# Delta rule and cross-attention: the gate's projection and Tanh moved among the level products, the state chain's last steps moved ahead of keys and taps, and stacks written whole to DRAM

## The reference

```python
def step(S, inp):
    qt, kt, vt, gt, bt = inp
    S = S * jnp.exp(gt)[..., None]
    vd = (vt - jnp.einsum('bhkv,bhk->bhv', S, kt)) * bt[..., None]
    S = S + kt[..., None] * vd[:, :, None, :]
    return (S, jnp.einsum('bhkv,bhk->bhv', S, qt))
...
q, k, v = (causal_conv_silu(x @ W, conv_w, conv_b) for each of q, k, v)   # 4 taps
g = -exp(A_log) * softplus(x @ Wfa @ Wfb + dt_bias)
q = l2norm(q) * SCALE; k = l2norm(k)
o = kda_scan(q, k, v, g, sigmoid(x @ Wb))
gate = (x @ Wga @ Wgb)
o = o * rsqrt(mean(o * o) + EPS) * o_norm_w * sigmoid(gate)
out = o @ Wo
```

## Time and profile before

| | |
|---|---|
| median of 3 runs | 6407.26 us (6398.27 to 6415.52) |
| the profiled execution | 6422.86 us |
| its span | 6421.3 us |
| PE / DVE / ACT / POOL busy | 78% / 61% / 43% / 32% of the span |
| granted clock of TensorE, mean | 0.911 of full speed |
| idle PE before L2223, all of the delta rule | 297.2 us |

### The profile page before, as it was taken

How to read it: one execution, slowest core, us unless ns; L and a number is a source line. 1 busy time by engine, 2 the same in 40 slices (tenths; PEclk the granted TensorE clock), 3 DMA queues, 4 the chain that set the end, 5 groups by cost and what they waited for, 6 DMA issues and landing times. The chain is left out here.

```text
span 6421.3 us, 83647 instructions
## 1 busy us (share of the span) xinstructions
PE 5027.0 (78%) x24879; PEld 3351.2 (52%) x24965; DVE 3933.4 (61%) x6588; ACT 2739.6 (43%) x4960; POOL 2059.8 (32%) x2623
## 2 busy tenths in 40 slices
PE   5789649998578888888888888888888765777656
PEld 3556425555355555666665556666555433444323
DVE  4676662222277766666766666677666245777756
ACT  5555451111134444444444444444444224777632
POOL 2456310201144444344444434344443132000100
PEclk8899869999689999999999999999999788999989
DMA  2011005344311111111111111111111012111110
GB/s 57 27 27 27 27 14 198 117 153 152 104 46 47 32 44 45 42 46 39 44 39 36 56 42 42 39 38 39 42 44 30 12 63 70 49 48 48 45 54 26
DMA packets 349801, 345.00 MB, mean 54 GB/s; under 512 B 99552, under 2 KB 252640, under 8 KB 348160
## 3 DMA queue, kind: packets, MB, share of 16 engines
q1 hardware_dynamic: 335472, 286.73, 15.1%
q0 software_dynamic: 13984, 54.01, 2.4%
HBM read 264.76 MB, written 75.89 MB: 53 GB/s over the span
## 5 line engine op out<-in xcount | busy, mean ns | idle before, releaser
L1810 POOL TENSOR_TENSOR delta_rule_suffix<-delta_rule_suffix,delta_rule_prefix 128x256 f32<-128x256 f32 x448 | 498.7, 1113 | 1213.0 <-ACT delta_rule_prefix L1904 766.7
L2150 PE MATMUL delta_rule_proj<-delta_rule_hT,delta_rule_w_qkv 128*128 128x512 f32 x1024 | 467.9, 600 | 0.0
L2174 PE MATMUL delta_rule_level<-delta_rule_qk_second,delta_rule_k_first 128*128 128x128 f32 x3072 | 425.6, 283 | 51.6 <-DVE delta_rule_L_small L1983 40.1
L1801 POOL TENSOR_TENSOR delta_rule_k_first<-delta_rule_qk,delta_rule_suffix 128x256 f32<-128x256 f32 x384 | 304.6, 793 | 495.5 <-PE delta_rule_level L2162 469.4
L2174 PEld LDWEIGHTS delta_rule_level<-delta_rule_qk_second,delta_rule_k_first 128*128 128x128 f32 x3072 | 385.8, 195 | 100.2 <-issue 78.2
L481 DVE TENSOR_TENSOR_SCAN scan_hs<-scan_decay,scan_inp 128x512 f32<-128x512 f32 x256 | 308.5, 1216 | 196.1 <-PE scan_inp L543 90.5
L2051 DVE TENSOR_TENSOR delta_rule_prefix<-delta_rule_prefix 128x256 f32<-128x256 f32 x448 | 286.8, 640 | 228.1 <-PE delta_rule_level L2162 189.0
L315 POOL TENSOR_TENSOR scan_hc<-scan_hs,scan_c_rows 128x512 f32<-128x512 f32 x256 | 334.5, 1312 | 283.8 <-DVE scan_hs L481 267.9
L2663 DVE TENSOR_REDUCE attend_top<-attend_scores 128x1 f32<-128x512 f32 x512 | 328.3, 683 | 131.2 <-DMA scan_c_rows<-bc_dram 85.5
L1994 DVE TENSOR_TENSOR delta_rule_qk_second<-delta_rule_qk,delta_rule_prefix 128x512 f32<-128x512 f32 x448 | 339.6, 758 | 47.4 <-issue 12.1
L1938 ACT ACTIVATE delta_rule_R<-delta_rule_inv 128x512 f32<-128x512 f32 x192 | 114.7, 597 | 568.7 <-PE delta_rule_inv L2209 568.7
(11 more groups left out here) (465 smaller groups left out, 11999.3 us busy)
## 6 DMA issues: line engine op xcount, KB each, us to landing
moe_w_d<-in_w_down SPq DMA_DIRECT2D x39, 512.0 KB, 4.4
scan_c_rows<-bc_dram SPq DMA_DIRECT2D x64, 256.0 KB, 3.8
delta_rule_w_qkv<-in_kda_wq SPq DMA_DIRECT2D x64, 256.0 KB
delta_rule_w_qkv<-in_kda_wk SPq DMA_DIRECT2D x64, 256.0 KB
delta_rule_w_qkv<-in_kda_wv SPq DMA_DIRECT2D x64, 256.0 KB
delta_rule_inv_beta<-beta_dram SPq DMA_DIRECT2D x64, 256.0 KB
delta_rule_w_o<-in_kda_wo SPq DMA_DIRECT2D x64, 256.0 KB, 4.8
small_dram<-delta_rule_L_small SPq DMA_DIRECT2D x64, 256.0 KB, 2.0
```

Source lines behind the costliest of these rows:

```text
L1801: pool.tensor_tensor(halves(k_first[:, i % 2, :], s, 0), halves(qk[p][:, 1, :], s, 0), first, ALU.mult).then_inc(k_ready, 1)
L1810: pool.tensor_tensor(first, first, whole_second, ALU.mult).then_inc(suffix_done, 1)
L2150: last = pe.matmul(to, w_qkv[p][:, i, k, :], hT[:, b % 2, k, :], start=(k == 0), stop=(k == DT - 1))
L2174: last = pe.matmul(level_ps[(i + 1) % 2][:, c, :], left, qk_second[:, i % 2, :, c * CHUNK // 2:(c + 1) * CHUNK // 2], start=True, stop=True)
```

## The change

Four constants and three places in the code are different.

1. `GATE_SLOT` goes from 4 to 18: the gate's projection on PE and its Tanh on ACT stand between the third step of the inverse and the level product of slot 18. Its weights have a function of their own, `load_gate`, which SP calls at the start of each iteration for the unit of that iteration instead of two iterations ahead inside `load_unit`.
2. On DVE the state after chunk 2 goes from slot 8 to slot 7 and `rhs` of chunk 3 from slot 9 to slot 8. The scaled keys get `KEY_SLOT` 7, behind that state, and the taps of v go from slots (7, 7, 9) to (8, 8, 9), behind that `rhs`. PE's and ACT's code of the back stage is the same.
3. `parts_dram` holds one slab for each of the 8 pairs, for q and for k: POOL stores 16 slabs a batch instead of 6, 64 in all instead of 24.
4. A head's stack is then one DMA of 128 rows for q and one for k, instead of three and three.

```diff
-        GATE_SLOT, NORM_K_SLOT = 4, 5
+        GATE_SLOT, NORM_K_SLOT = 18, 5
-        V_PROJ_SLOT, V_OUT_SLOT, CONV_V_SLOTS = 3, 6, (7, 7, 9)
+        V_PROJ_SLOT, V_OUT_SLOT, CONV_V_SLOTS = 3, 6, (8, 8, 9)
+        RHS_SLOTS, STATE_SLOTS, KEY_SLOT = (0, 3, 6, 8), (2, 5, 7), 7
...
-                    reach(sp, gate_done, n - 3)
-                    sp.dma_start(w_g[:, n % 4, :], g["kda_wgb"][:, cols]).then_inc(wg_loaded[n % 4], 16)
                     reach(sp, norm_scaled, n - 1)
...
+                def load_gate(n):
+                    h = n % HEADS
+                    reach(sp, gate_done, n - 3)
+                    sp.dma_start(w_g[:, n % 4, :], g["kda_wgb"][:, h * K:(h + 1) * K]).then_inc(wg_loaded[n % 4], 16)
...
                 for i in range(N + 4):
+                    if i < N:
+                        load_gate(i)
...
+                    elif slot == KEY_SLOT:
                         dve.wait_ge(k_scale_done, n + 1)
                         dve.tensor_tensor(qk[p][:, 1, :], qk[p][:, 1, :], k_scale[:], ALU.mult).then_inc(k_normed, 1)
...
-                            for part in range(PARTS):
-                                pool.dma_start(g["parts_dram"][w, part, bass.ds(2 * bb + half, 1)].rearrange("o c p s -> p (o c) s"),
-                                               parts[:, half, w, part, :, :]).then_inc(parts_stored, 16)
+                            for at, pair in enumerate(PART_PAIRS):
+                                pool.dma_start(g["parts_dram"][w, at, bass.ds(2 * bb + half, 1)].rearrange("o c p s -> p (o c) s"),
+                                               parts[:, half, w, pair[w], :, :]).then_inc(parts_stored, 16)
...
-                            sp.dma_start(q_stack[to, s, :], q_dram[a, bass.ds(n, 1), at, :].to_broadcast(
-                                [count, X_DIM, S])).then_inc(stack_loaded[s], 16)
-                            sp.dma_start(k_stack[to, s, :], k_dram[0:count, bass.ds(n, 1), at, :].rearrange(
+                        for stack, source in ((q_stack, q_dram), (k_stack, k_dram)):
+                            sp.dma_start(stack[:, s, :], source[:, bass.ds(n, 1), at, :].rearrange(
                                 "e o d s -> (e o) d s")).then_inc(stack_loaded[s], 16)
```

More of the change, by code:

```diff
@@ L2089, in back @@
                     p = n % 2
-                    if slot < 3 * CHUNKS:
-                        c, part = divmod(slot, 3)
-                        if part == 0 and c > 0:
-                            dve.wait_ge(from_state, (CHUNKS - 1) * n + c)
-                            dve.tensor_tensor(rhs[:], v_rows[n % 3][:, c, :], seq_ps[:, 0, :], ALU.subtract).then_inc(rhs_done, 1)
-                        elif part == 2 and c < CHUNKS - 1:
-                            dve.drain()
-                            dve.wait_ge(to_state, CHUNKS * n + c + 1)
-                            if c == 0:
-                                dve.tensor_copy(state[:, 0, :], seq_ps[:, 2, :]).then_inc(state_done, 1)
-                            else:
-                                dve.scalar_tensor_tensor(state[:, c % 2, :], state[:, (c + 1) % 2, :], decay_end[n % 4][:, c:c + 1],
-                                                         seq_ps[:, 2, :], ALU.mult, ALU.add).then_inc(state_done, 1)
+                    if slot in RHS_SLOTS[1:]:
+                        c = RHS_SLOTS.index(slot)
+                        dve.wait_ge(from_state, (CHUNKS - 1) * n + c)
+                        dve.tensor_tensor(rhs[:], v_rows[n % 3][:, c, :], seq_ps[:, 0, :], ALU.subtract).then_inc(rhs_done, 1)
+                    elif slot in STATE_SLOTS:
+                        c = STATE_SLOTS.index(slot)
+                        dve.drain()
+                        dve.wait_ge(to_state, CHUNKS * n + c + 1)
+                        if c == 0:
+                            dve.tensor_copy(state[:, 0, :], seq_ps[:, 2, :]).then_inc(state_done, 1)
+                        else:
+                            dve.scalar_tensor_tensor(state[:, c % 2, :], state[:, (c + 1) % 2, :], decay_end[n % 4][:, c:c + 1],
+                                                     seq_ps[:, 2, :], ALU.mult, ALU.add).then_inc(state_done, 1)
                     elif slot == GATED_SLOT:
@@ L2433, in _ @@
                             act.wait_ge(turned, 2 * t + w + 1)
-                            act.wait_ge(parts_stored, 16 * 2 * PARTS * (2 * bb + half - 1 if half else 2 * bb))
+                            act.wait_ge(parts_stored, 16 * 2 * len(PART_PAIRS) * (2 * bb + half - 1 if half else 2 * bb))
                             act.activation(parts[:, half, w, 0, :, at], turned_ps[w][:], ACT.Copy, scale=SCALES[w]).then_inc(first_done, 1)
@@ L2581, in _ @@
                         sp.wait_ge(scores_done, TPB * (n * H + j + 1))
-                        for a in range(PARTS):
-                            pairs = [pair for pair in PART_PAIRS if pair[0] == a]
-                            lo, count = PART_PAIRS.index(pairs[0]) * X_DIM, len(pairs)
-                            to = slice(lo, lo + count * X_DIM)
-                            sp.dma_start(q_stack[to, s, :], q_dram[a, bass.ds(n, 1), at, :].to_broadcast(
-                                [count, X_DIM, S])).then_inc(stack_loaded[s], 16)
-                            sp.dma_start(k_stack[to, s, :], k_dram[0:count, bass.ds(n, 1), at, :].rearrange(
+                        for stack, source in ((q_stack, q_dram), (k_stack, k_dram)):
+                            sp.dma_start(stack[:, s, :], source[:, bass.ds(n, 1), at, :].rearrange(
                                 "e o d s -> (e o) d s")).then_inc(stack_loaded[s], 16)
@@ L2591, in _ @@
                 for s in range(RING):
-                    sp.wait_ge(stack_loaded[s], 16 * 2 * PARTS * N * H // RING)
+                    sp.wait_ge(stack_loaded[s], 16 * 2 * N * H // RING)
             @block.gpsimd
@@ L2611, in score @@
                     m, s = n * H + j, j % RING
-                    pe.wait_ge(stack_loaded[s], 16 * 2 * PARTS * (n * (H // RING) + j // RING + 1))
+                    pe.wait_ge(stack_loaded[s], 16 * 2 * (n * (H // RING) + j // RING + 1))
                     for i in range(TPB):
@@ L3107, in program @@
     g["fg_dram"] = nc.dram_tensor("fg_dram", (B, P, 2, S), F32).ap()
-    g["parts_dram"] = nc.dram_tensor("parts_dram", (2, PARTS, B, DT, P, S), BF16).ap()
+    g["parts_dram"] = nc.dram_tensor("parts_dram", (2, len(PART_PAIRS), B, DT, P, S), BF16).ap()
     with Scope(nc, "main") as sc:
```

2 lines of the change are left out of this document (1 added, 1 removed).

## The result

The changed kernel takes 6179.36 us (median of 4 runs, 6177.75 to 6184.41), the kernel before 6406.32 us beside it on the same chip. The ratio is 0.9647, with a 95% interval of 0.963 to 0.9663: 3.5% faster. The forecast was 6172 us. The profiled execution took 6177.75 us (span 6176.2); 245.1 us of span are gone.

The account below looks back on a forecast made before the run. Bounds: PE's 4.33 us wait for DVE's state in each delta-rule unit, and SP's DMA issuing in the attention. 6422.9 - 204 + 34 - 65 = 6188 us, 15.6 above the median, so 6172; range 6072 to 6275.

Parts of the forecast that it names:

- State and `rhs` forward: Delta rule, DVE's order after chunk 2: PE gets the state earlier, so L2162 starts 3.5 us earlier in each unit.
- The clock: Delta rule, PE's half clock behind the wait: up to 1.75 us more a unit; 3.5 us taken as about the middle.
- The two bounds of 2.2 and 5.2: Delta rule, gain in us a unit: 2.2 if the clock falls for the same 6.8 us, 5.2 if it never falls.
- Gate out of slot 4 and into slot 18: Delta rule: chunk 1's chain comes 0.3 us earlier; the new place among the level products costs 0.1 us a unit.
- Delta rule in all: Delta rule's sum: 3.4 us a unit over the 60 units with the wait, -204 us; bounds -126 and -306.
- Stores: Cross-attention's projections, POOL's stores of 16 slabs: later landing and issuing add 34 us, at 1.6 us between stores.
- Two DMAs a head: Attention: fewer SP issues cut a head from 5.43 to 4.95 us, 61 us, plus 3.5 at the start: -65 us.
- 1: Delta rule: the clock no longer falls, since PE's idle piece is broken up; 6086 us, or 6070 beside the median; 20%.
- 2: Delta rule: the clock falls in every unit as before; 6266 us, or 6250 beside the median; 22%.
- 3: Attention stays at 5.4 us a head because landing of a 128-row stack, not its issue, is the bound; 6233 us; 5%.
- 4: Projections: stores follow each other only after landing, +280 us, 6452 us; decides from 5.4 us a store on; 3%.
- 5: Delta rule: slot edits do nothing, PE waits for something as late; gain 0.3 to 1 us a unit, 6340 us; 5%.

Follow-up runs that it names:

- the run without them: Changed kernel with a new batch's input loads issued one iteration later, where SP stores no solved matrices: 6172.85 us, ratio 0.964 to the kernel before.

## Why the prediction was right

By its own steps:

- **State and `rhs` forward: right, in its size too.** The state was to let PE go on 3.8 us earlier, and does 3.76 (from 22.92 to 19.16 us after the unit's start). The pieces of 0.8, 0.9 and 1.0 us came out as 0.80, 0.64 and 1.06, then 0.39 for the taps. L2162 was to be 3.5 us earlier and is 3.26.
- **The clock: the value was right, the mechanism was not.** I took 3.5 as a mean over a clock that falls in some units and not in others. It falls in every unit, for half as long. At the copy of RT a unit is 3.49 us ahead of before. The two bounds of 2.2 and 5.2 were set by "for the same 6.8 us" and "never"; a shorter stretch was not among the cases, and that the value fits is luck: the shorter stretch happens to cost what the middle does. The upper bound is borne out: with the clock kept up, units take 46.3 us, 4.9 less than 51.2, where I had 5.1 with the gate.
- The Trainium skill, "TensorE: Matmul & The Clock Gate", section on HAM oscillation, has the engine stay warm once the loop is reordered so that the wait does not come between the pieces of work. Here an order that took 3.5 of the 4.33 us from the wait did not do that: the pieces that are left still bring the clock down in each unit. Only the run with products in these pieces keeps 1.00.
- **Gate out of slot 4 and into slot 18: nothing net, as the sum had it nearly.** The chain of chunk 1 gained 0.23 us (0.3 in the prediction), the new place costs 0.09 (0.1), and the run with the gate alone shows no change: what comes earlier there only waits longer for DVE.
- **Delta rule in all: -197 us (193.3 + 4.1) for -204.** The difference is the long units: the run without them has 7.0 us less. The prediction does not ask what a shorter unit does to X's transfer; this term was missing.
- **Stores: +38.6 us between the first store and the first score, for 34 less the 3.5 that I counted at the attention's start, so 8 too few.** The interval of 1.6 us was right: landings lie 1.5 to 1.9 apart. Left out was POOL's stop. A batch on the path takes 30.7 us, not 27.5; without the stop the last store of the second batch would have landed about 1.5 us after 5097.69, so the stop costs 2.5 us there and about as much at the end. The two batches together are 6.4 of the 8 us; the rest was not traced to a step.
- **Two DMAs a head: mechanism right, size too small.** 61 us were to come from a cycle of 5.43 to 4.95. The cycle is 4.87, so (5.43 - 4.87) x 128 = 72 without the start's 3.5, and the run with six DMAs gives 78 in all. Between the two profiled executions it is 86, because that of before had heads of 5.52 us where the runs with six DMAs a head have 5.47. The Trainium skill ("DMA: Bandwidth & Descriptors", "Issuing engines are not separate DMA queues") has the time to initiate a DMA as usually small beside the DMA. The traces have no landing times for the stacks, so they can't say whether one issue of 0.73 us is small beside its DMA; but six of them a head set the cycle, and four or two do not, so what was forecast from that rule (no gain) did not come.

The two errors of the stacks cancel: the stacks alone took off 30.7 us where the sum had 31. That the sum lies so close to the measured time is luck in this part too. Of the rivals, 1 is out, since the clock falls. Of 2, the first half came true (it falls in every unit) and the price did not, since it falls for half as long. 3 (landing as the bound) is out, 4 needed 5.4 us a store and there are 1.6, and of 5 nothing is seen.

## What to carry to other kernels

Where an engine with work for two chains has a short step that another engine waits for, put that step right behind its operand and let the long steps of the other chain wait: a few slot numbers were worth 3% here. Count a wait's price with the clock behind it; if the wait can't go, products that nobody reads, in the gap, bring that part back. And when a queue's issuing is the bound, it is enough to get it below the engines' cycle: four DMAs a head gave the same 4.87 us as two, with five slabs fewer to store in each batch.

## What was not expected of the hardware

- POOL stops issuing after 15.4 to 15.9 MB of these stores (31 of 512 KB or 60 of 256 KB) until all have landed; 16.15, 15.21 and 10.61 us of idle time with no releaser in the profile.
- PE's idle pieces of at most 1.06 us, with 0.5 to 0.9 us of work between them, were enough for the granted clock to fall to 0.50 (1.2 GHz) in every unit.
- Eight small DMA issues of SP take 6.7 to 7.8 us behind the loads of a batch, and 2.9 to 4.2 us otherwise: the issue itself takes longer there. What holds it was not shown.
